# State-space stage: the upper half of the first factor left as two partial products that TensorE sums

## The reference

```python
dA = (1.0 + dtA / 2) / (1.0 - dtA / 2)
Ct = B[None] * C / (1.0 - dtA / 2) * dt[:, None]
l = jnp.arange(L)                       # L = 512
V = jnp.exp(jnp.log(dA)[:, :, None] * l)  # powers dA**l, complex
K = 2.0 * jnp.einsum('chn,hnl->chl', Ct, V).real
```

## Time and profile before

| | us |
|---|---|
| median of 3 runs | 1400.87 |
| lowest, highest | 1399.15, 1401.68 |
| the profiled execution, its own time | 1402.95 |
| its span in the profile | 1401.0 |
| state-space stage, to the first VectorE instruction of the next | 174.2 |
| VectorE's pace in the chunk loop | 14.28 a chunk |
| last product on TensorE | 154.97 to 160.66 |

### The profile page before, as it was taken

The page is one execution under the profiler, slowest core; times in us unless marked ns, Lnnn a source line. Parts: engine busy times, 40 slices in busy tenths (PEclk is TensorE's granted clock), DMA queues, the critical chain, the costliest instruction groups (busy, mean ns, idle before and its releaser), DMA issues. The chain is left out here.

```text
span 1401.0 us, 22789 instructions
## 1 busy us (share of the span) xinstructions
PE 1079.7 (77%) x5647; PEld 663.5 (47%) x5649; DVE 632.8 (45%) x1459; ACT 360.6 (26%) x1030; POOL 403.5 (29%) x583
## 2 busy tenths in 40 slices
PE   0443378888768888768997598989789889799965
PEld 0343367777657677633444243434334434344432
DVE  8999643554434544466877222222222222222221
ACT  2111044455335454422000022112111112121211
POOL 0000032022032122010048244444444444444533
PEclk9776689999989999979997799999999999899997
DMA  4144400000000000020041257656674776655583
GB/s 148 28 64 84 68 1 2 1 1 1 3 1 1 2 1 1 1 69 0 24 180 46 94 127 211 172 122 167 167 211 108 212 212 152 169 121 135 125 252 64
DMA packets 51114, 124.37 MB, mean 89 GB/s; under 512 B 21648, under 2 KB 22672, under 8 KB 46304
## 3 DMA queue, kind: packets, MB, share of 16 engines
q1 hardware_dynamic: 31824, 76.63, 17.2%
q0 software_dynamic: 19216, 46.82, 17.2%
HBM read 169.78 MB, written 35.44 MB: 146 GB/s over the span
## 5 line engine op out<-in xcount | busy, mean ns | idle before, releaser
L1447 PE MATMUL ex_gu<-ex_wt,ex_xT 128*128 x680 | 341.3, 626 | 23.0 <-issue 22.6
L1567 POOL DMA_INDIRECT out_dram<-ex_ys,ex_sidx x84 | 135.4, 1612 | 267.2 <-DMA out_dram<-ex_ys,ex_sidx 129.7
L1447 PEld LDWEIGHTS ex_gu<-ex_wt,ex_xT 128*128 128x128 f32 x680 | 121.9, 200 | 124.1 <-issue 124.1
L1484 PE MATMUL ex_y<-ex_wt,ex_actT 128*128 x336 | 157.9, 592 | 0.0
L1525 DVE TENSOR_SCALAR ex_gc<-ex_gu 128x256 f32<-128x256 f32 x84 | 35.6, 424 | 221.5 <-PE ex_gu L1447 220.9
L1506 ACT ACTIVATE ex_ys<-ex_y,ex_share 128x512 f32<-128x512 f32 x84 | 57.7, 687 | 259.8 <-PE ex_y L1484 249.7
L638 ACT ACTIVATE at_pg<-at_S,at_nmax 128x129 f32<-128x129 f32 (+1 forms) x256 | 104.9, 423 | 72.0 <-DVE at_nmax L750 65.3
L1529 DVE TENSOR_TENSOR ex_act<-ex_sil,ex_uc 128x256 f32<-128x256 f32 x84 | 35.8, 426 | 180.6 <-ACT ex_sil L1500 180.6
L750 DVE TENSOR_REDUCE at_nmax<-at_S 128x1 f32<-128x129 f32 (+1 forms) x256 | 81.9, 353 | 78.3 <-PE at_S L518 72.7
L1541 POOL DMA_INDIRECT ex_xg<-x_rows,ex_gidx x89 | 90.2, 1014 | 71.7 <-POOL ex_gidx L1538 71.7
L1438 PE MATMUL ex_tx<-ex_ident,ex_xg 128*128 128x128 f32 x344 | 56.3, 289 | 59.4 <-DMA ex_xg<-x_rows,ex_gidx 58.1
(11 more groups left out here) (303 smaller groups left out, 1949.6 us busy)
## 6 DMA issues: line engine op xcount, KB each, us to landing
ex_wt<-in_wexp_dram SPq DMA_DIRECT2D x85, 1536.0 KB
x_rows<-rt_xa SPq DMA_DIRECT2D x16, 272.0 KB
ssm_rows<-ssm_c SPq DMA_DIRECT2D x8, 512.0 KB, 3.8
H<-ssm_rows SPq DMA_DIRECT2D x16, 256.0 KB, 5.5
out_dram<-H SPq DMA_DIRECT2D x16, 256.0 KB
at_watt<-in_watt_dram SPq DMA_DIRECT2D x1, 1536.0 KB, 8.5
ex_xg<-x_rows,ex_gidx POOLq DMA_INDIRECT x89, 3.8
out_dram<-ex_ys,ex_sidx POOLq DMA_INDIRECT x84, 4.9
```

What stands on the lines that cost most here:

```text
L1447: last = M(gu[n % 2][:], xT[n % 2][:, kc, :], wt[:, bass.ds(base + kc * 2 * FF, 2 * FF)], start=(kc == 0), stop=(kc == KC - 1))
L1484: last = M(yb[n % 2][:], actT[:, c, :], wt[:, bass.ds(base + KC * 2 * FF + c * DM, DM)], start=(c == 0), stop=(c == FC - 1))
L1567: P.indirect_dma_start(T["acc"], bass.IndirectOffsetOnAxis(ap=sidx[n % 2][:], axis=0), ys[n % 2][:], None, compute_op=ALU.add).then_inc(sc ...
```

## The change

- The third level of v is not made. Columns 32 to 63 of v would be dA^32 times columns 0 to 31, whose real part is v_re z_re - v_im z_im and imaginary part v_im z_re + v_re z_im. ScalarE writes the two parts with z_re into columns 32 to 63, channel by channel, since its scale is one value per partition (`upper`, 16 ACTIVATEs a chunk of 64 elements). VectorE writes the two parts with -z_im and z_im into a new buffer `tz` of 32 columns, in two instructions over 16 channels.
- TensorE adds a second matmul for each one there was, with the same stationary operand and 32 columns of `tz`, into the upper half of the same PSUM region. A chunk has 128 matmuls for 64.
- VectorE's order changes: levels 0 and 1 of v, then a signal `half_ready` to ScalarE, then the two products into `tz`, then the three levels of q, then `powers_ready`. The waits that v and q shared are now each one's own.
- New waits: ScalarE for `half_ready`, TensorE for `upper_ready`, VectorE for the product two chunks back before it writes `tz` (and, once, for the class row's matmuls, whose work buffers one of the `tz` uses). A negated copy of z_im (`nz`) is made once.
- On ScalarE `upper(ch + 1)` stands ahead of the wait for product ch, and the small copies for chunk ch + 2 now stand ahead of the copy of result ch instead of behind it.

```diff
--- before.py
+++ after.py
@@ -86,7 +86,10 @@
         vb = [sb(f"ssm_v{n}", [128, 2, IC, LB]) for n in range(2)]
         qb = [sb(f"ssm_q{n}", [128, 2, IC, NCH, LA]) for n in range(2)]
         half = 2 * NI * NCH
-        tv = prod[:, 0:half].rearrange("q (r s i b) -> q r s i b", r=2, s=2, b=LB // 2)
+        tv = prod[:, 0:half // 2].rearrange("q (r s i b) -> q r s i b", r=2, s=2, b=LB // 4)
+        tz = [t.rearrange("q (s i b) -> q s i b", s=2, b=LB // 2) for t in
+              (prod[:, half // 2:half], wk[:, 0:8, :].rearrange("q k d -> q (k d)"))]
+        nz = wk[:, 9, :]
         tq = prod[:, half:2 * half].rearrange("q (r i c a) -> q r i c a", r=2, i=2 * IC, c=NCH)
         zq = sb("ssm_zq", [128, 3, 2, CHUNKS, 2 * IC])
         kb = [cri[:, n, :].rearrange("q (i b) -> q i b", b=LB) for n in range(2)]
@@ -101,6 +104,7 @@
         c_ready = sem("ssm_c_ready")
         preloaded = sem("ssm_preloaded")
         dve_step = sem("ssm_dve_step")
+        half_ready, upper_ready = sem("ssm_half_ready"), sem("ssm_upper_ready")
         z_ready, zq_ready = sem("ssm_z_ready"), sem("ssm_zq_ready")
         low_ready, low_copied = sem("ssm_low_ready"), sem("ssm_low_copied")
         powers_ready, prod_ready, prod_taken = sem("ssm_powers_ready"), sem("ssm_prod_ready"), sem("ssm_prod_taken")
@@ -170,14 +174,26 @@
             for b in range(2):
                 nc.scalar.activation(at["kT"][:, b, 0:1], cqk[:, 0:1], ACT.Identity, bias=bias[:, 4:5])
             nc.scalar.activation(cv, cqk[:, 128:256], ACT.Identity, bias=bias[:, 5:6]).then_inc(cls_act, 1)
+            def upper(ch):
+
+                n, i0 = ch % 2, ch * IC
+                act.wait_ge(half_ready, ch + 1)
+                for i in range(IC):
+                    last = nc.scalar.activation(vb[n][:, :, i, LB // 2:LB], vb[n][:, :, i, 0:LB // 2], ACT.Copy,
+                                                scale=z[:, 5, 0, i0 + i:i0 + i + 1])
+                last.then_inc(upper_ready, 1)
+
+            upper(0)
             for ch in range(CHUNKS):
                 n = ch % 2
+                if ch + 1 < CHUNKS:
+                    upper(ch + 1)
                 act.wait_ge(prod_ready, ch + 1)
+                if ch + 2 < CHUNKS:
+                    copy_low(ch + 2)
                 if ch >= 2:
                     act.wait_ge(k_stored[n], 16 * (ch // 2))
                 nc.scalar.copy(kb[n], ps[n][:]).then_inc(prod_taken, 1)
-                if ch + 2 < CHUNKS:
-                    copy_low(ch + 2)
 
         @block.vector
         def _(dve):
@@ -246,6 +262,7 @@
             done(V.tensor_tensor(q0[:, 1], tl[:, 0, 1], tl[:, 1, 0], ALU.add))
             dve.wait_ge(cls_rstd, 1)
             V.tensor_scalar(cx, cls, cst[:, 6:7], cst[:, 9:10], ALU.subtract, ALU.mult).then_inc(cls_xn, 1)
+            V.tensor_scalar(nz, z[:, 5, 1, :], -1.0, None, ALU.mult)
             V.memset(v0[:, 0, :, 0:1], 1.0)
             V.memset(v0[:, 1, :, 0:1], 0.0)
             for k in range(3):
@@ -268,21 +285,32 @@
                 dve.wait_ge(low_copied, 2 * ch + 2)
                 if ch == 0:
                     dve.wait_ge(zq_ready, 2)
-                for k in range(3):
-                    m, a = LOW << k, 1 << k
-                    for r in range(2):
-                        zz = zq[:, k, r, ch].unsqueeze(2).unsqueeze(3).to_broadcast([128, 2 * IC, NCH, a])
-                        V.tensor_tensor(tq[:, r, :, :, 0:a],
-                                        q[:].rearrange("q r i c a -> q (r i) c a")[:, :, :, 0:a], zz, ALU.mult)
+                for k in range(2):
+                    m = LOW << k
                     for r in range(2):
                         zz = z[:, 3 + k, r, i0:i0 + IC].unsqueeze(1).unsqueeze(3).to_broadcast([128, 2, IC, m])
                         last = V.tensor_tensor(tv[:, r, :, :, 0:m], v[:, :, :, 0:m], zz, ALU.mult)
                     done(last)
+                    V.tensor_tensor(v[:, 0, :, m:2 * m], tv[:, 0, 0, :, 0:m], tv[:, 1, 1, :, 0:m], ALU.subtract)
+                    done(V.tensor_tensor(v[:, 1, :, m:2 * m], tv[:, 0, 1, :, 0:m], tv[:, 1, 0, :, 0:m], ALU.add))
+                dve.sem_inc(half_ready, 1)
+                if ch >= 2:
+                    dve.wait_ge(prod_ready, ch - 1)
+                if ch == 1:
+                    dve.wait_ge(cls_pe, 4)
+                m = LB // 2
+                for s, factor in ((0, nz[:, i0:i0 + IC]), (1, z[:, 5, 1, i0:i0 + IC])):
+                    V.tensor_tensor(tz[n][:, s], v[:, 1 - s, :, 0:m], factor.unsqueeze(2).to_broadcast([128, IC, m]), ALU.mult)
+                for k in range(3):
+                    a = 1 << k
+                    for r in range(2):
+                        zz = zq[:, k, r, ch].unsqueeze(2).unsqueeze(3).to_broadcast([128, 2 * IC, NCH, a])
+                        last = V.tensor_tensor(tq[:, r, :, :, 0:a],
+                                               q[:].rearrange("q r i c a -> q (r i) c a")[:, :, :, 0:a], zz, ALU.mult)
+                    done(last)
                     re, im = slice(0, IC), slice(IC, 2 * IC)
                     V.tensor_tensor(q[:, 0, :, :, a:2 * a], tq[:, 0, re, :, 0:a], tq[:, 1, im, :, 0:a], ALU.add)
-                    V.tensor_tensor(q[:, 1, :, :, a:2 * a], tq[:, 0, im, :, 0:a], tq[:, 1, re, :, 0:a], ALU.subtract)
-                    V.tensor_tensor(v[:, 0, :, m:2 * m], tv[:, 0, 0, :, 0:m], tv[:, 1, 1, :, 0:m], ALU.subtract)
-                    done(V.tensor_tensor(v[:, 1, :, m:2 * m], tv[:, 0, 1, :, 0:m], tv[:, 1, 0, :, 0:m], ALU.add))
+                    done(V.tensor_tensor(q[:, 1, :, :, a:2 * a], tq[:, 0, im, :, 0:a], tq[:, 1, re, :, 0:a], ALU.subtract))
                 dve.sem_inc(powers_ready, 1)
 
             V.tensor_copy(at["identb"][:], at["ident"][:])
@@ -319,14 +347,18 @@
             for ch in range(CHUNKS):
                 n = ch % 2
                 pe.wait_ge(powers_ready, ch + 1)
+                pe.wait_ge(upper_ready, ch + 1)
                 if ch >= 2:
                     pe.wait_ge(prod_taken, ch - 1)
                 for i in range(IC):
                     for p in range(2):
                         h = slice(64 * p, 64 * p + 64)
                         for r in range(2):
-                            last = nc.tensor.matmul(ps[n][h, i, :], qb[n][h, r, i].rearrange("q c a -> q (c a)"), vb[n][h, r, i, :],
-                                                    start=(r == 0), stop=(r == 1))
+                            qs = qb[n][h, r, i].rearrange("q c a -> q (c a)")
+                            nc.tensor.matmul(ps[n][h, i, :], qs, vb[n][h, r, i, :], start=(r == 0), stop=False,
+                                             skip_group_check=True)
+                            last = nc.tensor.matmul(ps[n][h, i, LB // 2:LB], qs, tz[n][h, r, i, :], start=False, stop=(r == 1),
+                                                    skip_group_check=True)
                 last.then_inc(prod_ready, 1)
 
         @block.gpsimd
```

## The result

The changed kernel takes 1409.39 us (median of 20 runs), the kernel before 1401.89 (20 runs). The ratio is 1.0057, with a 95% interval of 1.0040 to 1.0074: slower by 0.6%, where 0.8% less was forecast. The profiled execution of the changed kernel took 1405.59 us, with a span of 1403.6.

The account below looks back on a forecast made before the run. VectorE was taken to bound the chunk loop, then the last product on TensorE. From 1402.95 us, minus 13.7 (VectorE) plus 3.0 (TensorE) gave 1392.2 profiled, or 1390.2 against the 1400.87 median; 8-in-10 range 1384.0 to 1396.5.

Parts of the forecast that it names:

- VectorE: In the chunk loop: net 1.74 us saved a chunk, pace 12.54 for 14.28, 13.7 us before the last product.
- the bounds set for the new waits: On VectorE in the chunk loop: at most 0.11 us more a chunk; if hidden, 3.5 us more gain.
- ScalarE: In the chunk loop: 16 small scaled ACTIVATEs, 0.31 us each, 5.0 us a chunk, costing nothing at a cover of 4 us.
- TensorE: In the chunk loop: the last product grows by 3.0 us to 8.7 on the path; the other seven are hidden.
- the clock: On TensorE: each product begins at half clock and ends at full; 3.8 us of the last at half, at most 5.6.
- the forecast's own dearest price: On TensorE: a 32-column record costs as much as a long one, 53 ns at half clock and 29 at full.
- the bound of 11.4: In the chunk loop: longest hidden product, 12.5 us pace less 1.1 us for ScalarE's two small copies after it.
- the short record at half clock: On TensorE: a 32-column record taken at 40 ns, the middle between 27 and 53.
- the 10.2 that it named as the most: On TensorE: longest product in us, with 5.6 us at half clock and the dearest record prices.
- The rule weighed there: On TensorE: some 60 cycles overhead a matmul, 50 ns at 1.2 GHz; last product about 8.9 us, predicted time 0.2 later.
- The cover: In the chunk loop: the longer product stays hidden in the first seven chunks, with 1.2 us spare at the worst mixture.
- The first came: Rival in the chunk loop: TensorE becomes the bound at half clock, 14.0 us a product, 1405.7 us; chance 0.06.

## Why the prediction was wrong

**VectorE: right.** 12.65 us a chunk for 12.54, 12.8 us before the last product for 13.7 (the run without the second matmul). The 0.1 us a chunk between them lies within the bounds set for the new waits.

**ScalarE: right.** 0.25 us each for 0.31 taken, 3.93 us a chunk, done 7 us before TensorE takes up that product in the change. The 93 ns of the Trainium skill, page "ScalarE: Activation LUTs", gave 0.24, nearer than my own value.

**TensorE: wrong, and this is the step that failed.** It had two prices. The first was the clock: "a longer product leaves it more time to" rise. It was taken from eight products of one kind of record and carried over to another kind. In the change the clock stood at 0.50 from the first product's start to the last one's end, with the engine busy for 116.7 of 117.5 us. With the short records at the forecast's own dearest price this was enough to lose the whole gain: at 0.50 and 53.4 ns a record (halves in turn, 8 columns) a product takes 13.8 us, over the bound of 11.4, and the next stage starts at 176.4, later than the 174.2 before. The second was the short record at half clock, taken as 40 ns, the middle between half of a long one and all of it. Eight records take 0.453 us. With the long ones at their 53.4 the short ones cost 60, above the upper bound of 53. That bound was too low because it left out the order: four matmuls in a row on one half cost 56.7 ns a record, halves in turn 53.4 (with 64 columns at full clock 36 and 29). At full clock, too, the short ones cost as much as the long (29.2 ns, halves in turn), where 25 was taken. With both prices a product is 14.7 us. Where the clock does rise (halves in turn, 9.2 to 10.7 us) it lies nearer the forecast's 8.7 than the change's 14.7, with a few products above the 10.2 that it named as the most.

The rule weighed there, that one column lasts as long as 60 (the Trainium skill, page "TensorEngine Tiling (Array Packing)", section "Instruction Overhead"), gave 50 ns at half clock. 8 and 32 columns cost the same in both orders, so the trace agrees with the rule, though at 53.4 ns and more and not 50, and the middle value I took against it was the wrong choice. By itself this would have cost little: the forecast's own sum with the dearest prices and a clock that rises was 10.2 us, within the bound of 11.4.

**The cover.** The bound of 11.4 us for a product was right as a mechanism: at 14.7 us VectorE waits 3.66 us, later 2.0, at a chunk's start for the small copies, and the pace is TensorE's. Products of up to 12.1 us in the 64-column run still went with a pace of 12.7, since only one was that long.

**The rivals.** The first came, which had a chance of 0.06: if "the clock stayed at half through a product and the short records cost as the long", 14.0 us and 1405.7. Measured are 14.7 us and 1409.4. Its chance hung on "the clock rose within each of the eight products", which was no evidence for another mixture of records. That the pause between products vanishes was foreseen in direction only; I had it help the clock.

**What stays open.** That the loss is the second matmul's is shown from both sides (without it 13.0 us are gained at the next stage, alone it costs 17.6). That the clock costs 11.0 of the 18.2 us between the change and its reordered form is shown by the 8-column run in the same order, if 8 and 32 columns cost the same there at half clock, as the starts of the records say. What in the array holds the clock down is not settled: it rose with wider second matmuls in one order and with halves in turn at 32 columns, and stayed down at 8 in either; TensorE was busy for nearly all of the time in the kernels in which it stayed down (116.7 of 117.5 us in the change, 109.5 of 109.6 with 8 columns in turn, 103.2 of 109.6 in the kernel before with the second matmul). That a short record pays for its weight load, and not for another fixed step, is only argued: the run meant for it met the change of width.

## What to carry to other kernels

A matmul that is added to an engine with idle time is free only at the clock that the engine will then have: price the new mixture at half clock too, and see whether the sum still fits; here 14.7 us did not fit into 11.4. Count short matmuls by their number, not by their columns (8 and 32 columns cost the same here), and let neighbouring ones use different parts of the array, which here was worth 18 us at the next stage with the same matmuls. When two engines' work is moved in one change, measure the parts: ScalarE's part alone, without the extra matmuls, gained 0.6% at the median, about as much as the forms of the whole whose clock rises (0.5 to 0.7%). Their next stage does start earlier (164.5 to 165.4 for 167.0), but the medians do not tell these 2 us apart.

## What was not expected of the hardware

- The granted clock stayed at 0.50 for 117.5 us in which TensorE was busy for 116.7, and with 64 or 48 columns for 32 in the second matmul, zeros included, it rose and the kernel was faster.
- The same 128 matmuls of a chunk in another order: with 8 or 32 columns in the short ones 56.7 or 53.4 ns a record at half clock, with 64 columns 36 or 29 at full.
- A change between parts of the array 64 and 32 wide: 0.21 us each time (one run).
